# Attention's instruction streams written out, and two groups of DMAs moved, in a fused two-layer kernel

## The reference

```python
xn = layernorm(x)                                       # after layer 0
s = L1_attn_ref(xn, gamma, beta, Wq, Wkv, Wo)           # 16 heads of 64, below
g = silu(L1_ffn_ref(xn, Wr, br, Wl1, bl1, Wl2, bl2, b)) # 8 experts, the best 2 of each token
return x + s * g

def _L1_attn_ref(x, gamma, beta, Wq, Wkv, Wo):
    q, k, v = heads(norm(x) @ Wq), heads(norm(x) @ Wkv) ...
    q, k = apply_rope(pos, q) * SCALE, apply_rope(pos, k)
    sim = where(causal_mask, neg, einsum('bhid,bhjd->bhij', q, k))
    return einsum('bhij,bhjd->bhid', softmax(sim), v) ... @ Wo

def apply_rope(pos, t):
    return t * cos(pos) + rotate_half(t) * sin(pos)
```

## Time and profile before

| what | value |
|---|---|
| time, median of 3 runs | 2537.87 us (2536.57 to 2540.17) |
| profiled execution, its own time | 2541.84 us |
| its span, first to last instruction | 2540.1 us |
| mean granted clock of TensorE | 0.957 |
| first attention | about 800 to 1784 us |
| second attention | about 2166 us to the end |
| busy: PE, PEld, DVE, ACT, POOL | 91%, 65%, 55%, 37%, 35% |

### The profile page before, as it was taken

The page is one execution under the profiler, slowest core; times in us unless marked ns, Lnnn a source line. Parts: engine busy times, 40 slices in busy tenths (PEclk is TensorE's granted clock), DMA queues, the critical chain, the costliest instruction groups (busy, mean ns, idle before and its releaser), DMA issues. The chain is left out here.

```text
span 2540.1 us, 57833 instructions
## 1 busy us (share of the span) xinstructions
PE 2318.2 (91%) x20696; PEld 1650.9 (65%) x20697; DVE 1393.2 (55%) x3950; ACT 935.6 (37%) x2197; POOL 899.5 (35%) x659
## 2 busy tenths in 40 slices
PE   7999999999977898989999999997999999797876
PEld 5555555666665566656677666766999999465554
DVE  6766242222257865657777777784333333474655
ACT  3211111111125353544556555553222222454452
POOL 4002002444455364554444344440111111446552
PEclk9999999999988898999999999998999999898987
DMA  6013104965456243343323333344777675343442
GB/s 213 17 50 116 50 17 144 267 203 160 110 139 211 74 118 97 97 132 105 81 74 74 92 103 83 95 108 164 246 234 243 234 243 177 100 140 103 113 118 68
DMA packets 158647, 331.09 MB, mean 130 GB/s; under 512 B 25057, under 2 KB 95217, under 8 KB 148049
## 3 DMA queue, kind: packets, MB, share of 16 engines
q1 hardware_dynamic: 137472, 284.98, 36.6%
q0 software_dynamic: 20944, 42.94, 6.5%
HBM read 193.61 MB, written 67.12 MB: 103 GB/s over the span
## 5 line engine op out<-in xcount | busy, mean ns | idle before, releaser
L1670 ACT ACTIVATE at_p<-at_p,at_nmax 128x640 f32<-128x640 f32 (+7 forms) x512 | 393.0, 770 | 224.0 <-DVE at_nmax L1902 221.8
L1902 DVE CUSTOM_DVE_ANT_0 at_p<-at_ps,atk_mask 128x512 f32<-128x512 f32 (+3 forms) x512 | 281.6, 582 | 183.4 <-PE at_ps L1606 159.6
L1606 PE MATMUL at_ps<-kept_big 64*128 64x512 f32 (+3 forms) x1536 | 299.2, 526 | 82.7 <-POOL kept_big L1726 42.7
L1920 DVE STREAM_TRANSPOSE at_pB<-at_p 128x512 f32<-128x512 f32 (+3 forms) x512 | 279.2, 585 | 156.5 <-PE at_ps L1627 150.0
L1720 POOL TENSOR_TENSOR kept_big<-kept_xg,atk_cos 128x1024 f32<-128x1024 f32 x64 | 151.3, 2364 | 389.2 <-ACT kept_xg L1695 385.5
L1591 PE MATMUL at_ps<-atk_h,atk_w 128*128 128x512 f32 x512 | 242.3, 617 | 32.0 <-DVE kept_big L1939 19.5
L1627 PE MATMUL at_ps<-at_pB,at_v_blocks 32*64 32x256 f32 (+1 forms) x8192 | 241.2, 362 | 25.6 <-issue 18.5
L1606 PEld LDWEIGHTS at_ps<-kept_big 64*128 64x128 f32 x1536 | 136.9, 196 | 190.8 <-issue 83.0
L1627 PEld LDWEIGHTS at_ps<-at_pB,at_v_blocks 32*64 32x64 f32 x8192 | 195.1, 141 | 89.9 <-issue 78.6
L1939 DVE SCALAR_TENSOR_TENSOR kept_big<-at_ps,at_inv,kept_big 128x256 f32<-128x256 f32 x512 | 203.6, 475 | 25.7 <-PE at_ps L1648 25.7
L1065 PE MATMUL ex_ps<-kept_big 128*128 128x512 f32 x480 | 210.2, 596 | 0.9 <-ACT kept_big L1122 0.9
(11 more groups left out here) (249 smaller groups left out, 3694.2 us busy)
## 6 DMA issues: line engine op xcount, KB each, us to landing
moe_w<-in_w_w SPq DMA_DIRECT2D x53, 1028.0 KB
kept_xg<-kept_xg SPq DMA_DIRECT2D x256, 128.0 KB, 3.0
at_v_blocks<-atk_first_w SPq DMA_DIRECT2D x512, 64.0 KB, 2.0
atk_first_w<-in_w_w SPq DMA_DIRECT2D x18, 1028.0 KB
atk_w<-in_w_qkv SPq DMA_DIRECT2D x32, 384.0 KB, 3.4
slot_in<-kept_big SPq DMA_DIRECT2D x9, 1032.0 KB
kept_big<-in_w_eg SPq DMA_DIRECT2D x16, 512.0 KB
kept_big<-in_w_eu SPq DMA_DIRECT2D x16, 512.0 KB
```

What stands on the lines that cost most here:

```text
L1606: pe.matmul(banks[e][:, 0:to - at], qkT[x][e * DH:(e + 1) * DH, n * P:(n + 1) * P], qkT[x][e * DH:(e + 1) * DH, T + at:T + to], start=True ...
L1670: act.activation(buf, buf, ACT.Exp, bias=nmax[:, unit:unit + 1], scale=-1.0, accum_out=rsum[:, unit:unit + 1]).then_inc(exp_done, 1)
L1902: ins = dve.tensor_tensor_reduce(out=p[unit % LAG][:, at:to], in0=ring[BANK_OF["S", (t, c), e]][:, 0:to - at], in1=mask[:, 0:CH] if to <= ...
L1920: dve.transpose(strided(pB[e][:, t * P:(t + 1) * P], TURN_STEP, keys), tiles(p[unit % LAG][:, 0:keys * P], keys)).then_inc(turned, 1)
```

## The change

Three edits. TensorE and ScalarE go through the same `run(act_on)` as VectorE, in which a plain Python loop writes all pairs out, so no loop and no register is left in their attention. In the first attention GpSimd does both rotations of a pair, then `end` if a sequence is over, and only then all eight sends; the count of later stages' semaphores moves behind the rotations too. In the second attention SyncE loads group 0 ahead of the pairs, and from then on, in each pair, stores group pr-1 and loads group pr+1 between the load of w and the replication, behind the swaps.

```diff
-        def run(eng, act_on):
+        def run(act_on):
+            pairs = nb * PAIRS
             act_on("first", -1, -1, 1, -1)
-            if nb > 1:
-                for u in range(2):
-                    act_on("both", u, u, u, 0)
-                with eng.Fori(1, PAIRS // 2) as i:
-                    for u in range(2):
-                        act_on("both", i * 2 + u, i * 2 + u, u, 0)
...
-            act_on("both", it + PAIRS - 2, PAIRS - 2, 0, nb - 1)
-            act_on("last", it + PAIRS - 1, PAIRS - 1, 1, nb - 1)
+            for it in range(pairs):
+                act_on("both" if it < pairs - 1 else "last", it, it % PAIRS, it % 2, it // PAIRS)
...
+                    close_load(0)
                     for pr in range(PAIRS - 1):
                         load_w = d.w["qkv"][(pr + 3) * P:(pr + 4) * P, :] if pr + 3 < PAIRS else None
-                        pair(pr, pr % 2, load_w, wo_of(pr + 1), then=lambda: close_load(pr))
-                        close_store(pr - 1)
-                    sp.wait_ge(w_ps, (PAIRS - 1) * 4 + ONE)
-                    close_load(PAIRS - 1)
+                        def next_group():
+                            close_store(pr - 1)
+                            close_load(pr + 1)
+                        pair(pr, pr % 2, load_w, wo_of(pr + 1), ready=next_group)
...
                         rotate(of, 0)
-                        if of == TOP * B + 1:
-                            for stage in ("moe", "at2"):
-                                d.signals[stage].count(pool)
+                        rotate(of, 1)
+                        if of > 0 and of % PAIRS == 0:
+                            end(of // PAIRS - 1)
...
-                            send(j, range(0, TB // 2))
-                        rotate(of, 1)
-                        if of > 0 and of % PAIRS == 0:
-                            end(of // PAIRS - 1)
-                        if 0 <= j < TOP * B:
-                            send(j, range(TB // 2, TB))
+                            for n in range(TB):
+                                pool.indirect_dma_start(out=d.xd, out_offset=..., in_=rows[j % 2][:, n * ROW:(n + 1) * ROW], in_offset=None).then_inc(sent, 16)
+                        elif j == TOP * B:
+                            for stage in ("moe", "at2"):
+                                d.signals[stage].count(pool)
```

More of the change, by code:

```diff
@@ L1416, in replicate, with pair @@
                                          v_top[b * QR:(b + 1) * QR, :]).then_inc(blocks_in, 16)
-                def pair(it, u, load_w, load_wo, half_free=lambda half: None, then=lambda: None, ready=lambda: None):
+                def pair(it, u, load_w, load_wo, half_free=lambda half: None, ready=lambda: None):
                     sp.wait_ge(w_ps, it * 4 + ONE)
                     sp.dma_start(wo[1 - u][:, :], load_wo).then_inc(wo_in[1 - u], 16)
-                    then()
                     for half in range(2):
@@ L1651, in act_on @@
                             last.then_inc(w_ps, 1)
-                run(pe, act_on)
+                run(act_on)
             @block.scalar
@@ L1726, in rotate @@
                     pool.tensor_tensor(out=out, in0=out, in1=other, op=ALU.add).then_inc(rot_done, 1)
-                def send(of, ns):
-                    for n in ns:
-                        at = of // B * NT + of % B * TB + n
-                        pool.indirect_dma_start(out=d.xd, out_offset=bass.IndirectOffsetOnAxis(ap=d.tok_slot[:, at:at + 1], axis=0),
-                                                in_=rows[of % 2][:, n * ROW:(n + 1) * ROW], in_offset=None).then_inc(sent, 16)
                 def end(b):
@@ L1948, in act_on @@
                                 dve.tensor_tensor(out=xa, in0=part_y, in1=xa, op=ALU.add).then_inc(out_done, 1)
-                pairs = nb * PAIRS
-                act_on("first", -1, -1, 1, -1)
-                for it in range(pairs):
-                    act_on("both" if it < pairs - 1 else "last", it, it % PAIRS, it % 2, it // PAIRS)
+                run(act_on)
                 dve.wait_ge(w_added, nb * (16 * PAIRS) + 16 + ONE)
```

15 lines of the change are left out of this document (3 added, 12 removed).

## The result

The changed kernel took **2503.3 us** (median of 4 runs, 2493.43 to 2509.75), the kernel before 2537.22 (median of 4). The ratio is 0.9863, with a 95% interval of 0.9827 to 0.9899. That is faster by 34 us, where 104.6 were forecast, and outside the range of 2394 to 2478. The profiled execution took 2505.49 us with a span of 2503.7.

What follows compares the result with a forecast made beforehand. TensorE's matmuls, about 34 us a pair, were taken as the bound, with excess elsewhere recoverable. Terms -14.3 - 41.3 - 3 - 1 + 7 - 52 = -104.6 took the span from 2540.1 to 2435.5; predicted median 2433 us, range 2394 to 2478.

Steps and rivals of the forecast that it cites:

- D: First attention: V0 is slow without the sends' doing and keeps its 13 us wherever they stand; 2473, chance 0.07.
- Edit 1: Stretches 9, 11, 13, 17, 19: without loops the jump's wait behind W goes; 184.3 to 170, -14.3 us.
- C: Gap behind W is VectorE's after all, so its 19.5 us and the lost clock stay; 2455, chance 0.05.
- Edit 2: Stretches 0 to 5: all eight sends behind the second rotation free V0 and the late scores; -41.3 us.
- x: Cost per first-attention stretch of sends beside V1, S4, W and A; taken as 4.5 us, between 0 and 10.
- rival B: First attention: sends hold TensorE as long as they run, 10 us a stretch; 2472, chance 0.13.
- Stretch 7: Eight sends instead of four ahead of the rotation's sum make TensorE idle 7 us; +7 us with the clock's fall.
- The first pass: Ahead of stretch 0: its slow V0 gains 6.5, the sends' new place costs 3.5; -3 us.
- Edit 3: Stretches 24 to 29: closing loads behind the swaps end the waits for the rotation; 35.3 each, -52 us.
- E: Second attention: store's wait and loads push the replication until V0 waits, half the gain; 2459, chance 0.09.
- heavier traffic in V0, 0.5: Stretches 24 to 29: allowance of 0.5 us a stretch for the moved closing loads' traffic in V0.
- rival F: All pairs: written-out TensorE code is fetched beside bulk DMAs and starves it at each 16 KB block; 2563, chance 0.03.

Runs made afterwards that it cites:

- s1_added_sends: Changed kernel with eight more indirect sends in each of six stretches without sends, 8 bytes or 1 KB a row; 2581.7 us, ratio 1.0158.
- e3_close: Kernel before with only the closing loads moved one group ahead, behind the swaps, on the chip without the hold; 2436.4 us, ratio 0.9806.
- e1_run: Kernel before with only TensorE's and ScalarE's attention written out, on the chip without the hold; 2465.4 us, ratio 0.9916.
- e4_run_close: Kernel before with written-out attention and moved closing loads, sends as before, on the chip without the hold; 2433.1 us, ratio 0.9784.
- e8_thin_load: Changed kernel with closing loads of groups 2 to 7 carrying 8 of 128 rows, same number of transfers; 2492.6 us, ratio 0.9799.
- h3_close: Kernel before with only the closing loads moved one group ahead, behind the swaps, on a chip with the hold; 2493.0 us, ratio 0.9811.

## Why the prediction was wrong

- **The reading of the bound** held: V0 at 13 us and the late scores stopped are the sends' doing, not V0's own. The rival that V0 is slow without them (D) is out: with the sends moved away V0 takes 6.1 to 6.6 us, and in s1_added_sends pairs that were clean become slow with added ones.
- **Edit 1** was right in place and nearly in size: -13.1 for -14.3 in its five stretches, -11.3 with the pauses of 0.7 to 1.3 us that written-out code has in others. Of the eight waits behind W none is left at its place; the one that remains is that of stretch 4, 2.62 us beside four sends. So C is out too.
- **Edit 2 is the step that failed: x.** "I take 4.5, a stall of the late-scores kind and part of V1 at half clock, since three quarters of the sends fall on W and A". Measured is x = 268.7 / 6 - 34 = **10.8**, rival B and a little over its bound of 10. The fault is in the reason: W and A were taken to be as free under sends as in stretch 7. Stretch 7 did not show that: A kept its place there, but ScalarE stood still for 3.95 us beside the same four sends and the transposes behind A for 1.25. On the chip without the hold (e3_close) ScalarE has no such gap in stretch 7. And W cannot start before ScalarE has V1's result; in stretches 1, 2 and 4 that is handed over late, and in the others V1 itself is drawn out, so the sends that were to run beside W run beside a TensorE that stands still or crawls. What counts is not which matmuls run beside a send but whether the next ones need something freshly handed over. The term comes to -3.6 for -41.3. The first pass, forecast at -3 by the same x, came to +3.5. Stretch 6 came as forecast. Stretch 7 came in size (+7.4 for +7) but not as reasoned: the wait for the rotation is 5.01 us, and the two pauses beside the sends, 2.7 in sum, made up the difference.
- **Edit 3** was right in mechanism and by itself nearly in size: -49 and -45 alone, for -52. TensorE waits neither for the rotation nor for the replication in 24 to 29, so E is out. The step that failed is "heavier traffic in V0, 0.5". Beside written-out code of TensorE it was 1.8 to 4.7 us in each of five stretches, with the clock behind them: 38.6 a stretch for 35.3, so -31.9. This is rival F's mechanism. F was priced at 1 us for every block of the kernel; it acts at few of them: 26 packets of code move in stretches 8 to 14, and a pause over 0.6 us stands behind two. In the changed kernel it reaches 1.8 us and more only where 2 MB pass beside the end of a stretch; in e1_run and e4_run_close, on the chip without the hold, it does so in stretches 0 to 5 too (2.7 and 3.0 us at most), beside the sends and the row loads. The Trainium skill ("Runtime: NRT & Kernel Launch", Instruction fetch mechanics) puts the crossing of a 16 KB block down as mostly hidden, and names jumps as a reason to write code out. The trace agrees on the jumps; on the crossing it agrees for most blocks, and not for those in V0 and V1: up to 0.8 us with the DMA engines idle, 1.8 to 4.7 with the closing loads beside them.
- Together: against their forecasts the terms came out 37.7 higher (stretches 0 to 5), 20.1 (24 to 29), 6.5 (first pass), 3.0 (8 to 21), 0.4 (7) and 0.5 (the rest), 68.2 in sum. 2433.3 + 68.2 = 2501.5, against 2503.3 measured.
- The range was too narrow because the two faults were treated as rivals of which one would come, while they stand in different stages and both came. B alone, at 2472, lay inside it; F, with a chance of 0.03, did not.

## What to carry to other kernels

To price an operation in a new place, ask what is handed over beside it, not only which engine is busy: two or three indirect sends at a time were free beside long projections, and a run of eight cost its whole length where TensorE's next work needed a fresh result of ScalarE. Before taking a row as proof that something is free, look at the other engines in that row's window too. Split such a run and put the pieces where there is slack (eight in a row cost 11 us, two by two 2.5). And where code is written out, keep bulk loads away from the stretches with the shortest instructions, since the next code can come late there.

## What was not expected of the hardware

- Of the four chips of the experiments, one shows no hold: the kernel before takes 2485.7 us there and 2538 to 2543 on the others, 2% apart. Each chip was used in one session, so it is not shown that the chip, and not something else about that session, makes the difference. e3_close and h3_close are the same kernel on either kind of chip, 57 us apart: 50.3 of them are in stretches 0 to 5 and 7.2 in the time ahead of the first. A verdict on the sends' place taken on that chip (0.9988) and on another (1.0053) differ in sign.
- An indirect send of GpSimd, 1.28 us from one to the next, holds what TensorE hands to ScalarE and VectorE on three of the four chips, with 8 bytes a row as with 1 KB. The Trainium skill ("SBUF — State Buffer", Who interferes with whom) says that DMA does not contend with a compute engine for its memory ports; that the bytes don't matter agrees with it, and the hold must be something else. What it is stays open: whether TensorE itself stops or its signals travel late can't be told, since the ends of matmuls in the profile are modelled, and what differs on the one chip is not known.
- TensorE goes on 1.3 to 1.5 us after its code has come, and beside bulk loads the code comes late: up to 4.66 us of standstill, with the DMA engines at 97.7% ahead of the packet. With fewer bytes in the same transfers (e8_thin_load) the longest standstill of these stretches is 1.1 us.
